# A graph network's gated messages: the gathered rows added by VectorE over whole PSUM banks, instead of by TensorE through an identity matmul

## The reference, cut to what matters

```
edge_input = concatenate([x[src], edge_attr], axis=-1)       # 96 + 32 features per edge
messages   = gelu(edge_input @ mW1 + mb1) @ mW2 + mb2
gates      = sigmoid(gelu(edge_input @ gW1 + gb1) @ gW2 + gb2)
aggregated = segment_sum(messages * gates, dst)
update     = gelu(concatenate([x, aggregated]) @ uW1 + ub1) @ uW2 + ub2
```

## Time and profile before

| What | Value |
|---|---|
| median of 3 runs | 5535.12 us (5534.68 to 5539.58) |
| profiled execution, its own time | 5541.19 us |
| its span in the trace | 5539.4 us |
| PE / PEld busy | 4218.1 us (76%) / 2623.9 us (47%) |
| DVE / ACT / POOL busy | 3559.9 us (64%) / 2445.4 us (44%) / 2862.0 us (52%) |
| the pass `sum_pass` | from 1690 us to 3910 us of the span |
| mean granted TensorE clock in the pass | 0.77 of full speed |
| DMA share in the pass | 0.38 of 16 engines, 117 GB/s |

### The profile page before, as it was taken

One profiled execution on the slowest core, in us unless ns is written; L12 is line 12 of the kernel. 1 busy time (PEld: TensorE's weight loads), 2 busy tenths in 40 slices (PEclk: granted clock), 3 DMA queues, 4 the chain that ended last, 5 costly groups with the idle time before them and its releaser, 6 DMA issues.

```text
span 5539.4 us, 95571 instructions
## 1 busy us (share of the span) xinstructions
PE 4218.1 (76%) x35389; PEld 2623.9 (47%) x35389; DVE 3559.9 (64%) x5454; ACT 2445.4 (44%) x4232; POOL 2862.0 (52%) x2968
## 2 busy tenths in 40 slices
PE   4777799999986555555555565565469999999998
PEld 3777699989973332333332333333433333333333
DVE  6999843354444544445444444444389999999999
ACT  4766600010002222223222232222258888888887
POOL 3100000000015666666666666666428888888887
PEclk9999999999987777777777777777689999999999
DMA  3333498969853333333333333433111212122121
GB/s 69 128 151 151 173 373 338 397 256 379 345 212 95 120 119 119 118 121 118 112 119 119 119 120 118 127 111 119 40 34 56 63 56 62 57 58 63 56 63 37
DMA packets 296278, 760.10 MB, mean 137 GB/s; under 512 B 81000, under 2 KB 183464, under 8 KB 289704
## 3 DMA queue, kind: packets, MB, share of 16 engines
q1 hardware_dynamic: 217352, 595.36, 29.5%
q0 software_dynamic: 78624, 160.79, 10.4%
HBM read 589.77 MB, written 166.22 MB: 136 GB/s over the span
## 4 chain that ended last, share of the span: by engine, by line
PE 40%; POOL 26%; issue 12%; DVE 11%; another core or an unknown queue 6%; DVEq 2%; ACT 2%; DMA 1%; SPq 0%; ACTq 0%; POOLq 0%
POOL GA L764 25%; PE p_e L1133 14%; PE p_tr L1280 9%; PE p_e L1265 9%; PE p_mm L1242 3%; DVE VA L2295 2%; PE p_mm L1052 1%; DVE R L1815 1%; DVE M L1817 1%; DVE GA L1817 1%; POOL VA L862 1%; DVE VA L1815 1%; DVE R L1817 1%; PE p_tr L1039 1%
## 5 line engine op out<-in xcount | busy, mean ns | idle before, releaser
L764 POOL DMA_INDIRECT GA<-table_mg,VA x1568 | 1489.0, 950 | 1745.7 <-DMA table_mg<-VA 987.1
L862 POOL TENSOR_SCALAR VA<-VA 128x1024 f32<-128x1024 f32 (+1 forms) x1204 | 1236.3, 1046 | 271.1 <-ACT VA L1567 257.9
L2295 DVE TENSOR_TENSOR VA<-VA,p_mm 128x2048 f32<-128x2048 f32 x602 | 1360.2, 2280 | 20.0 <-POOL VA L862 17.3
L1165 PE MATMUL p_e<-BD,EA 128*128 128x384 f32 x896 | 411.9, 609 | 576.4 <-ACT GA L1515 522.6
L2097 DVE TENSOR_TENSOR M<-GA,p_mm 128x1344 f32<-128x1344 f32 x112 | 174.1, 1554 | 977.2 <-ACT GA L1515 831.3
L1567 ACT ACTIVATE VA<-p_e 128x1024 f32<-128x1024 f32 x602 | 616.6, 1024 | 199.1 <-PE p_e L1265 199.0
L1280 PE MATMUL p_tr<-VA,GA 128*32 128x512 f32 (+1 forms) x5096 | 641.5, 580 | 4.2 <-ACT GA L1587 2.1
L1171 PE MATMUL p_e<-GA,C 128*128 128x384 f32 x896 | 431.6, 640 | 252.2 <-DMA GA<-table_mg,VA 221.1
L2123 DVE SCALAR_TENSOR_TENSOR R<-R,keep,M 128x97 f32<-128x97 f32 x1568 | 512.7, 327 | 139.3 <-issue 26.1
L1515 ACT ACT_TABLE_LOAD x112 | 143.7, 1283 | 954.5 <-remote 751.2
L1165 PEld LDWEIGHTS p_e<-BD,EA 128*128 128x128 f32 x896 | 202.5, 236 | 760.6 <-issue 627.8
(11 more groups left out here) (267 smaller groups left out, 7035.3 us busy)
## 6 DMA issues: line engine op xcount, KB each, us to landing
GA<-adj SPq DMA_DIRECT2D x98, 800.0 KB, 6.1
VA<-adj SPq DMA_DIRECT2D x98, 800.0 KB, 6.1
run_m<-R SPq DMA_DIRECT2D x112, 700.0 KB
GA<-adj SPq DMA_DIRECT2D x98, 768.0 KB, 6.2
VA<-adj SPq DMA_DIRECT2D x98, 768.0 KB, 6.2
H<-adj SPq DMA_DIRECT2D x56, 896.0 KB, 5.1
adj<-GA SPq DMA_DIRECT2D x25, 1568.0 KB, 5.2
adj<-VA SPq DMA_DIRECT2D x24, 1568.0 KB, 5.1
```

Source lines behind the costliest of these rows:

```text
L764: pool.indirect_dma_start(out=to, out_offset=None, in_=of, in_offset=bass.IndirectOffsetOnAxis(ap=at, axis=0)).then_inc(s, 16)
L862: pool.tensor_scalar(e, e, HIGH, LOW, ALU.min, ALU.max).then_inc(clipped, 1)
L1165: mm = pe.matmul(p_h[k][0:CH, 0:4 * D], EA[:, h, k // 2, :], BD[:, 2 * (k % 2):2 * (k % 2) + 2, :, :].rearrange("p a b f -> p (a b f)"), s ...
L2295: dve.tensor_tensor(e, e, p_mm[n % 2][:, 0:cols_of(n)].unsqueeze(1).to_broadcast([P, HEADS, cols_of(n)]), ALU.mult).then_inc(weighed, 1)
```

## The change: what it does

The edge products stay on TensorE, but close their sums at once (`stop=True`), and the identity matmuls are gone. VectorE reads the banks in two operations instead: banks 0 to 3 with slots 0 to 7 of `G` (1536 elements per partition), and banks 4 to 6 with slots 8 to 13 (1152 elements), and writes the sum to `A`. Each raises `rows_added`. ScalarE takes gelu in place in `A`, in two operations of the same sizes. The gate product is made in place in `A`. GpSimd waits for `rows_added` of batch n-2 where it waited for `hidden_ready`; TensorE waits for `rows_added` of the batch before where it waited for `gelu_done`; `edge_product` is raised twice per batch and has a new reader, VectorE. For that the four single banks `p_tr` and `p_mm` become one allocation of four banks, `p_front`.

```diff
--- before.py
+++ after.py
@@ -322,12 +322,14 @@
         rec = small[:, 0, 0:GRP * HEADS].rearrange("p (t e) -> p t e", t=GRP)
         Wqk = W[:, 0:3, :].rearrange("p n f -> p (n f)")[:, 0:2 * P].rearrange("p (k f) -> p k f", k=2)
 
-        p_tr = [ps(f"p_tr{k}", [P, 512]) for k in (0, 1)]
-        p_mm = [ps(f"p_mm{k}", [P, 512]) for k in (0, 1)]
+        p_front = ps("p_front", [P, 4, 512])
+        p_tr = [p_front[:, k, :] for k in (0, 1)]
+        p_mm = [p_front[:, 2 + k, :] for k in (0, 1)]
         p_c = [*p_tr, *p_mm]
         p_four = ps("p_e", [P, 4, 512])
         p_e = [p_four[:, k, :] for k in range(4)]
         p_h = [*p_e, *p_tr, p_mm[0]]
+        hid_p = [p[0:CH, 0:n, 0:4 * D].rearrange("p k (a f) -> p k a f", a=2) for p, n in ((p_four, 4), (p_front, BANKS - 4))]
         p_pair = p_four[:, 0:2, :]
         p_last = [p_e[HEADS - 1], p_tr[1]]
         p_sums = p_tr[0]
@@ -335,6 +337,7 @@
         gates = p_mm[1][0:CH, D:D + U]
         p_top = p_e[3]
         n_top = len(BOUNDED) + 1
+        part_of = [slice(0, 8), slice(8, U)]
         pairs = [(g, c) for g in range(UG) for c in (0, 1) if EG * g + 2 * c < U]
         assert len(pairs) == BANKS
 
@@ -389,8 +392,8 @@
         nodes_settled = sem("nodes_settled")
         sources_landed = sem("sources_landed")
         rows_landed = [sem(f"rows_landed{h}") for h in (0, 1)]
-        hidden_ready = sem("hidden_ready")
-        sums_ready = [sem(f"sums_ready{h}") for h in (0, 1)]
+        rows_added = sem("rows_added")
+        sums_made = sem("sums_made")
         sums_stored = [sem(f"sums_stored{h}") for h in (0, 1)]
         ends_landed = [sem(f"ends_landed{g}") for g in range(GROUPS)]
         open_ready = sem("open_ready")
@@ -597,14 +600,14 @@
 
                 def load_batch(k):
                     if k >= 2:
-                        sp.wait_ge(edge_product, k - 1)
+                        sp.wait_ge(edge_product, 2 * (k - 1))
                     sp.dma_start(EA[:, k % 2, :, :], edge_t[:, UG * k:UG * (k + 1), :]).then_inc(edge_landed[k % 2], 16)
                 load_batch(0)
                 load_batch(1)
                 for k in range(BATCHES):
                     if k + 2 < BATCHES:
                         load_batch(k + 2)
-                    sp.wait_ge(sums_ready[k % 2], k // 2 + 1)
+                    sp.wait_ge(sums_made, k + 1)
                     sp.dma_start(by_chunk(run_m)[:, U * k:U * (k + 1), :], R[:, k % 2, :, :]
                                  ).then_inc(sums_stored[k % 2], 16)
 
@@ -798,7 +801,7 @@
                 pool.wait_ge(table_stored, 16 * GROUPS * 2)
                 for k in range(2 * ITER):
 
-                    wait(pool, hidden_ready, BANKS * (k - 1))
+                    wait(pool, rows_added, 2 * (k - 1))
                     for j in range(U):
                         gather(G[0:CH, k % 2, j, 0:2 * D], table_mg, sources[:, U * k + j:U * k + j + 1],
                                rows_landed[k % 2])
@@ -1159,19 +1162,15 @@
                 for n in range(BATCHES):
                     h = n % 2
                     pe.wait_ge(edge_landed[h], 16 * (n // 2 + 1))
-                    for k in range(BANKS):
-
-                        wait(pe, gelu_done, BANKS * (n - 1) + k + 1)
-                        mm = pe.matmul(p_h[k][0:CH, 0:4 * D], EA[:, h, k // 2, :],
-                                       BD[:, 2 * (k % 2):2 * (k % 2) + 2, :, :].rearrange("p a b f -> p (a b f)"),
-                                       start=True, stop=False)
-                    mm.then_inc(edge_product, 1)
-                    pe.wait_ge(rows_landed[h], 16 * U * (n // 2 + 1))
-                    for k in range(BANKS):
-                        pe.matmul(p_h[k][0:CH, 0:4 * D].rearrange("p (a f) -> p a f", a=2), C[0:CH, C_ID:C_ID + CH],
-                                  G[0:CH, h, 2 * k:2 * k + 2, 0:2 * D], start=False, stop=True
-                                  ).then_inc(hidden_ready, 1)
-                pe.wait_ge(gelu_done, BANKS * BATCHES)
+                    for part, banks in enumerate((range(0, 4), range(4, BANKS))):
+
+                        wait(pe, rows_added, 2 * (n - 1) + part + 1)
+                        for k in banks:
+                            mm = pe.matmul(p_h[k][0:CH, 0:4 * D], EA[:, h, k // 2, :],
+                                           BD[:, 2 * (k % 2):2 * (k % 2) + 2, :, :].rearrange("p a b f -> p (a b f)"),
+                                           start=True, stop=True)
+                        mm.then_inc(edge_product, 1)
+                pe.wait_ge(sums_made, BATCHES)
                 close_and_update()
 
             def scatter_pass(n):
@@ -1509,12 +1508,9 @@
             def sum_pass():
                 for n in range(BATCHES):
                     h = n % 2
-                    wait(act, sums_ready[h], n // 2)
-                    for k in range(BANKS):
-                        act.wait_ge(hidden_ready, BANKS * n + k + 1)
-                        act.activation(A[0:CH, h, 2 * k:2 * k + 2, :],
-                                       p_h[k][0:CH, 0:4 * D].rearrange("p (a f) -> p a f", a=2), ACT.Gelu
-                                       ).then_inc(gelu_done, 1)
+                    for part, of in enumerate(part_of):
+                        act.wait_ge(rows_added, 2 * n + part + 1)
+                        act.activation(A[0:CH, h, of, :], A[0:CH, h, of, :], ACT.Gelu).then_inc(gelu_done, 1)
                     gate(n, gates)
 
             def scatter_pass(n):
@@ -2109,20 +2105,30 @@
 
                 for n in range(BATCHES):
                     h = n % 2
+                    dve.wait_ge(rows_landed[h], 16 * U * (n // 2 + 1))
+                    for part, of in enumerate(part_of):
+                        dve.wait_ge(edge_product, 2 * n + part + 1)
+                        dve.tensor_tensor(A[0:CH, h, of, :].rearrange("p (k a) f -> p k a f", a=2), hid_p[part],
+                                          G[0:CH, h, of, 0:2 * D].rearrange("p (k a) f -> p k a f", a=2), ALU.add
+                                          ).then_inc(rows_added, 1)
+                    dve.wait_ge(gelu_done, 2 * (n + 1))
+                    gate_part = A[0:CH, h, :, D:2 * D]
+                    dve.tensor_tensor(gate_part, gate_part, gate_row.unsqueeze(1).to_broadcast([CH, U, D]), ALU.mult)
                     dve.drain()
-                    dve.wait_ge(gelu_done, BANKS * (n + 1))
-                    gated(n, A[0:CH, h, :, :], gate_row, gates)
-
+                    dve.tensor_reduce(small[:, 0, 0:U], gate_part, AX_X, ALU.add).then_inc(logit_ready, 1)
+                    dve.wait_ge(gate_ready, n + 1)
+                    dve.tensor_tensor(M[:, :, 0:D], A[0:CH, h, :, 0:D], gates.unsqueeze(2).to_broadcast([CH, U, D]),
+                                      ALU.mult)
+                    dve.tensor_copy(M[:, :, D:MW], gates.unsqueeze(2))
+                    wait(dve, sums_stored[h], 16 * (n // 2))
                     for j in range(U):
                         before = R[:, h, j - 1, 0:MW] if j else R[:, 1 - h, U - 1, 0:MW]
-                        step = U * n + j
+
                         dve.drain()
-                        if j == 0:
-
-                            wait(dve, sums_stored[h], 16 * (n // 2))
-                        op = dve.scalar_tensor_tensor(out=R[:, h, j, 0:MW], in0=before, scalar=keep[:, step:step + 1],
-                                                      in1=M[:, j, 0:MW], op0=ALU.mult, op1=ALU.add)
-                    op.then_inc(sums_ready[h], 1)
+                        op = dve.scalar_tensor_tensor(out=R[:, h, j, 0:MW], in0=before,
+                                                      scalar=keep[:, U * n + j:U * n + j + 1], in1=M[:, j, 0:MW],
+                                                      op0=ALU.mult, op1=ALU.add)
+                    op.then_inc(sums_made, 1)
 
                 def open_nodes(g):
```

## The result

| What | Before | After |
|---|---|---|
| median (range, runs) | 5536.40 us (5529.53 to 5544.89, 7) | 5556.93 us (5551.65 to 5562.78, 7) |
| ratio, 95% interval | | 1.0034 (1.0025 to 1.0044) |
| span of the profiled execution | 5539.4 us | 5555.5 us |
| PE / DVE / ACT busy | 4218.1 / 3559.9 / 2445.4 us | 3761.2 / 3895.6 / 2401.8 us |
| first release to the last message gather | 2185.6 us | 2202.2 us |

The kernel became slower by 20 us. The forecast was 170 us (5705), with 5590 as its lowest end: the sign was right, the size eight times too large.

The account below looks back on a forecast made before the run. It took GpSimd's gather pauses, ended by held TensorE updates, as the bound. Longer pauses +152.9, start +4.2 and end +13 us made +170 on 5535, so 5705 us, range 5590 to 5800.

Parts of the forecast that it names:

- What bounds the kernel: Edge pass: GpSimd's gathers pause because TensorE's updates are held beside unbroken gathers and let go together 4.27 us after GpSimd stops.
- The pauses are therefore what there is to win: GpSimd in the edge pass: without pauses a batch takes 17.6 us, so the pauses cost 2.3 us per batch.
- Follow one pause: Edge-pass cycle: second batch's products held, both additions exposed, so a 7.8 us pause every two batches; 2338.5 us for 2185.6, +152.9.
- The twelve microseconds: TensorE's updates in the edge pass: seen at once for some 12 us after GpSimd resumes, then held.
- the forecast's cycle: Edge pass: 28 gathers in 34.86 us, then a 7.8 us pause, for every two batches.
- VectorE's 3.11 us come behind it, in the open: Each pause: both VectorE additions, 3.11 us, follow the held update with all engines waiting; pause 4.27 + 0.1 + 3.11 + 0.3 = 7.8 us.
- a first product that always gets out early: Uncertainty in the pause: if the first of two products always leaks out, its 1.74 us addition is hidden, -94 us.
- The rival of lengthening runs: Edge pass: leaked products let GpSimd run four batches, halving payments of 3.4 us addition and restart; 5644 down to 5590; chance 0.16.
- Start and end: Pass edges: first release +4.2 us; after the last gather two batches still to add, 37.3 us for 24.6, +13.
- Prices: Per batch: additions 1.74 and 1.37 us, three-bank products 3.84, gelus 1.46 and 1.14 behind a 1.28 table load; VectorE's batch 16.5.
- The rival of no holding: Edge pass: pauses were TensorE's own late matmuls, so removing them lets GpSimd issue unbroken, -250 us, 5285 us; chance 0.11.

Follow-up runs that it names:

- e12: Kernel after with the edge pass emptied to gathers alone (110 of 112 batches of messages left out), slow chip: 5457.85 us beside 5543.39 for the kernel before.
- e13: Kernel after with one edge-product update per batch, behind the seventh bank, instead of two; slow chip: 5613.11 us, 1.0114 of the kernel before.
- e17: Kernel after with VectorE's additions of the next batch moved ahead of the running sums; slow chip: 5550.75 us, 0.9982 of the kernel before.
- e9: Kernel after, every second batch's last edge product forced to wait for the next batch's rows, both additions behind it; slow chip: 5648.87 us, 1.0203 of before.
- e5: Kernel after, word for word, on a quick chip: 5265.34 us beside 5263.51 for the kernel before, ratio 1.0008.
- e15: Kernel after with all but the first two batches' loads, products, gelu, additions and sums left out, slow chip: 5458.31 us beside 5559.36 for the kernel before.
- e14: Kernel after with edge products made for the first batch only, VectorE adding the same banks every batch; slow chip: 5541.18 us, 0.9997 of the kernel before.
- e18: Kernel before with one hidden_ready update per batch, behind the last identity matmul, instead of seven; slow chip: 5573.40 us, 1.0020 of the unchanged kernel before.
- e16: Kernel after with message gathers moving half of each row's bytes, as many rows; slow chip, one run: 5590.83 us beside 5559.36 for the kernel before.

## Why the prediction was right or wrong

One rule covers the slow chips: **n gathers occupy n x 1.40 us, whoever waits, and what a cycle costs beyond this is the work that begins only after the wait.** It holds from one full pause to the next. A run whose pause ends early leaves its debt to the next: in the kernel after, the runs of 41 end 2.0 us under 41 x 1.40 (8 runs) and those of 14 run 4.5 over theirs (9 runs). Start of a run to start of the next, less n x 1.40, as a median over the most frequent kind of run:

| Kernel | n (runs) | beyond n x 1.40 | what is in the open |
|---|---|---|---|
| e12 | 112 (12) | -0.02 us | nothing |
| before | 28 (31) | 0.59 us | GpSimd's restart |
| after | 42 (20) | 1.67 us | one addition, 1.35, and the restart |
| e13 | 42 (21) | 3.41 us | both, 1.75 + 1.35, and the restart |
| e17 | 42 (15) | 0.00 us | nothing: the second addition starts 1.6 us before the 58.8 are over |
| e9 | 28 (54) | 2.28 us | both; the product itself ends 1.1 us before the 39.2 are over |

In the 20 runs of 42 of the kernel after the held addition starts 0.05 us, in the median, behind the moment at which 58.8 us are over. Over the whole pass 1540 gathers at 1.40 make 2156.0 us; the kernel before stands 29.6 above this, the kernel after 46.2.

- **What bounds the kernel: half right.** Updates held beside unbroken gathers, let go together: yes. "The pauses are therefore what there is to win" was wrong on the chip of the result. The 0.17 us per gather that the prediction read from 2.46, 4.81 and 7.03 us was mostly a debt (1.40 - 1.25 = 0.15) that every gather leaves and that a pause pays off; the rest is the usual 0.30 us between two gathers. Its own rows say this: 39.67 us for 28 gathers is 1.42 each. The floor is 19.6 us per batch for the 19.87 measured, not 17.6; only 0.3 us could be won.
- **The step that failed: "Follow one pause".** It said of the products of m+2, "20 and more after GpSimd resumed: held. GpSimd runs its second batch out". They passed: the products that end at 3042.66 were read at 3048.43. The twelve microseconds came from one late row and were made a limit. The third batch's were held, so a cycle has 42 gathers, not 28. With the forecast's cycle, 34.86 + 7.8 = 42.66 us for 28 gathers, a batch costs 21.33; measured was 20.02 over the pass. For the pass that is 152.9 us forecast against 16.6. About half of this error is the length of the runs: with 42 gathers and both additions in the open (e13's cycle, 62.2 us) a batch is 20.74, some 65 us less over 110 batches. The next point is the other half: 60.5 us per cycle, 20.16 per batch, some 64 us less again. (Both are estimates from medians.)
- **"VectorE's 3.11 us come behind it, in the open": half of it.** VectorE, free since the running sums ended at 3071.20, had made its first addition already, since that product (3055.25) had passed while the second (3057.19) had not. 1.35 us stay in the open instead of 3.11. The prediction had named this case, a first product that always gets out early, and priced it at -94 us, but did not count on it. e13 puts both there, and its ratio is 1.0114 where the kernel after has 1.0034. That the time rose at all has the reason that the prediction gave, an addition behind a held update. But it needed the chip: on a quick one even the sign fails (e5, 1.0008, with 1 in its interval).
- **What the forecast's own cycle costs** is shown by e9: 41.5 us for 28 gathers and +109 us. By the rule it is 39.2 + 3.11 + 0.3 = 42.6, so the price of the pause was fair, for a pause that the kernel after doesn't have.
- **The rival of lengthening runs** (0.16) is nearest to what happened: three batches to a run where it had four. It had the floor in a weaker form ("the pace cannot fall below the present one") and came to 5590 to 5644, because it left both additions in the open and kept 17 us for start and end.
- **Start and end: too large.** GpSimd's first gather, its first release, its last message gather and its first gather of `run_m`:

```profile
1633.88 0.98 POOL L767 DMA_INDIRECT GA<-table_mg,VA  x1 [982.65 <-DMA table_mg<-VA]
...
1697.07 0.94 POOL L767 DMA_INDIRECT GA<-table_mg,VA  x1 [28.44 <-DVE GA L2111]
...
3898.32 0.95 POOL L767 DMA_INDIRECT GA<-table_mg,VA  x1 [0.30 <-issue]
...
3928.61 0.94 POOL L767 DMA_INDIRECT VA<-run_m,ends  x1 [29.34 <-DMA run_m<-R]
```

The release comes 63.2 us after the first gather; before, 1699.69 - 1637.62 = 62.1: +1.1 for the +4.2 forecast. At the end the forecast had two batches behind the last gather, +13; the gap is 29.34 us for 28.3 before: batch 110 had been added before the gathers stopped. Sum of the measured terms: 16.6 + 1.1 + 1.0 = 18.7 us. They come from one execution of each kernel, whose spans differ by 16.1 us (5555.5 and 5539.4); the medians differ by 20.5.
- **Prices.** Additions 1.75 and 1.35 us for 1.74 and 1.37: right. Products of three banks 3.81 us behind a pause (3081.46), as the 3.84 forecast, and 2.1 to 2.5 otherwise. ScalarE's pair of gelus 2.54 us for 2.60, but the table load is not in its path:

```profile
3034.81 2.54 ACT L1513 ACTIVATE GA<-GA 128x1536 f32<-128x1536 f32 x2 [7.78 <-DVE GA L2111]
3037.37 1.28 ACT L1506 ACT_TABLE_LOAD   x1
3040.60 0.28 ACT L1506 ACTIVATE p_front<-small,sc 128x14 f32<-128x14 f32 x1 [1.95 <-issue]
3040.89 1.28 ACT L1513 ACT_TABLE_LOAD   x1
```

The gelu's table is loaded right behind the sigmoid, in ScalarE's idle time. VectorE's batch is so 15.4 us (3033.03 to 3048.43) and not 16.5. No pause hung on it.
- **The rival of no holding** (0.11, 5285 us) is wrong on the slow chips. On the quick ones nothing is held, but in neither kernel (5263 and 5265 us), so the gain of 250 us that it gave to the change is seen nowhere.

Not settled: what takes the 1.40 us; why one product passes late in a run and the next doesn't, and why in e17 the held one passes before the 58.8 us are over; and why the kernel before took 5543 us beside e12 and 5559 beside e15, on the same chip.

## What to carry to other kernels

When a pause grows in proportion to the work ahead of it, divide the whole cycle, not the busy part, by the number of items. If that quotient is constant (1.42 us per gather over 28 here), the pause is a debt of the resource, and neither removing the wait (e14) nor fewer updates (e18) changes much. Charge a moved operation only for what starts after the debt is paid, and put it where it can be done earlier, as e17 does. And never make a limit out of one late row: find the row that passed last as well.

## What the runs showed of the hardware

- The same kernel takes 5263 us on some chips and 5536 to 5559 on others. Indirect gathers of 128 rows of 768 bytes leave every 1.25 us on the first, and need 1.40 on the second, with 384 bytes as well (60.8 us per 42 in e16); GpSimd may be 26 to 28.5 us ahead (e12) before its own record stretches from 0.95 to 1.10 us.
- While it is ahead, TensorE's updates are late, by 22.9 us in the kernel after and by 43 us in e12. The packets are not: one gather outstanding in the kernel after, in e12 and on a quick chip alike.
- While it is ahead by some microseconds, VectorE's dependent steps (a drain and a 0.32 us operation) come one per 1.40 us and not per 0.40: 252 of 1456 steps of the kernel after take over 1.2 us, and 10 of the kernel before. In e5 and e9 none takes over 0.9.
